# Last pair's edge columns copied on chip; edge products and folds laid between the halves of the convolutions

## The chip, the cores and the metric

The kernel runs on one core of one Trainium2 chip. The time is device microseconds (us) of one execution, the median of several. TensorE (PE in the profile) multiplies, VectorE (DVE), ScalarE (ACT) and GpSimd (POOL) do the work around it, SyncE (SP) issues transfers. Each engine takes its own instructions in the order in which they are written, and engines meet at semaphores.

## What is computed

Two levels are applied to `x`, 32 samples of 64 channels and 1024 columns. Each level is a style-modulated stack of four one-dimensional convolutions (same, upsample with blur, same, blur with downsample), then a feed-forward part whose result is added to `x`. Cut to what matters:

```python
def cond(x, style, weights, biases, mod_w, mod_b):   # one level's convs
    for i, typ in enumerate(('same', 'upsample', 'same', 'downsample')):
        x = _layer(x, style, weights[i], biases[i], mod_w[i], mod_b[i], typ)
    return x
...
x = x + L0_ffn(L0_cond(x, cond_512, ...), A, B, Wr)        # top-16 of 64 adapters of rank 16
x = x + L1_ffn(L1_cond(x, cond_512, ...), qweight, scales, zeros, bias)  # int4 weights, y = s*(q.x) - z*sum(x) + bias
```

The second level's input is the first level's output, sample by sample.

## The kernel before

**Work and tiles.** Two samples make a pair, 16 pairs a level, numbered 0 to 15 in level 0 and 16 to 31 in level 1. A pair's `x` is 128 rows (two samples of 64 channels) by 1024 columns, with even and odd columns apart, so that a convolution of one sample is a product over 128 rows (64 channels, even and odd) and 512 columns. Every float32 operand is split into a rounded part (`hi`) and a remainder (`lo`), and a product is three matmuls (hi-hi, hi-lo, lo-hi).

**Steps of a pair `c`**, by the functions of the code. `a` is the half, that is the sample, 0 or 1.
- `split`: ACT writes `x_hi`, DVE writes `x_lo` of both samples from `x_in`.
- `layer1(c, a)`: the first conv, 6 matmuls of 512 columns into `conv_ps[a]`; then ACT scales in place and writes `h_hi`, then DVE writes `h_lo` (`dve_layer1`, two instructions).
- `fold3(c)` (6 matmuls of 384) and `fold2(c)` (15 of 256): these combine the pair's remaining three convs into one set of weights. `fold_start` is the ACT and DVE work ahead of `fold3` (`v_hi`, `v_lo`). After `fold3` come `r_hi`, `r_lo`, after `fold2` come `e_hi`, `e_lo` (three ACT and three DVE instructions).
- `cond(c, a)`: the folded convs, 12 matmuls of 512 columns; ACT then writes `cond` with `act_cond`.
- `turn`, then `adapter_out` (level 0) or `quant` (level 1): 8 transposes, and the feed-forward products, 24 matmuls of 512 for each half in level 0, 16 for each in level 1. `rowsum` follows `quant`; then DVE adds bias and zero terms in `dve_second_residual`.

**Edges.** Folded convs are wrong in the first and last column. These are computed apart, for all 32 samples at once, from `x_edge`, the few outer columns of each sample: `edge_vector` steps 0 to 4 on DVE alternate with `edge_tensor` layers 0 to 3 on PE (6, 12, 6 and 18 small matmuls). Layer `k` on PE needs step `k` on DVE, which needs layer `k-1` on PE. `act_ends` copies the result into `cond`.

**Order at the change of level.** Level 1 runs three pairs ahead (`AHEAD = 3`), so pairs 16, 17, 18 and 19 go through their convs before pair 16's `quant`. Loops run over pairs 1 to 13 of level 0 and, three at a time, over pairs 17 to 28 of level 1. Between the loops everything is written out by hand. There the level-1 edge chain runs too, and level 1's weights (`quant`) are unpacked from nibbles by eight DVE and eight ACT instructions. Level 1's edge chain needs `x_edge` of all samples, so the last pair's level-0 result too: DVE writes it to `res` (`dve_first_residual`), POOL stores it to `x_scratch` in HBM (`x_after_first` in the trace), and SP loads the outer columns back with four transfers (`edge_loads`).

```python
def edge_loads(sp, s, samples):
    ...
    sp.dma_start(s.x_edge[0:C, 0, samples, 0:4], src[:, :, 0, 0:4]).then_inc(S.edges_loaded, 16)
```

The functions that the change touches follow, as they stand in the kernel before.

Of the kernel before, what the change touches and what calls it, by code (L numbers as in the profile page):

```python
# [18 lines left out]
B, C, D = 32, 64, 1024  # L19
STYLE = 128  # L20
P = 128
NPAIR = B // 2
H = D // 2
# [11 lines left out]
AHEAD = 3  # L35
# [4 lines left out]
def program(nc, t):  # L40
    with ExitStack() as outer:
        def sem(name):
            return outer.enter_context(nc.semaphore(name))
# [30 lines left out]
        S = Buffers()  # L74
        S.link = sem("link")
        S.edges_clear = sem("edges_clear")
        S.edges_loaded = sem("edges_loaded")
        S.ident_ready = sem("ident_ready")
# [190 lines left out]
        EDGES_LOADED = (16, 16 + 2 * 4 * 16)  # L269
# [189 lines left out]
        def edge_vector(v, L, s, step):  # L459
# [12 lines left out]
            if step == 0:  # L472
                V.memset(s.edge[1][hi_half, 0, 0, :], 0.0)
                V.memset(s.edge[1][lo_half, 1, 2, :], 0.0)
                v.wait_ge(S.edges_loaded, EDGES_LOADED[L])
                for side in range(2):
# [506 lines left out]
        def _(sp):  # L983
# [42 lines left out]
            edge_loads(sp, set1, slice(B - 2, B))  # L1026
# [12 lines left out]
        def _(pool):  # L1039
# [42 lines left out]
            pool.wait_ge(S.x1_stored, 16 * NPAIR)  # L1082

# [34 lines left out]
        def _(pe):  # L1118
# [74 lines left out]
            c = NPAIR + 2  # L1193
            pe.wait_ge(S.x1_ready, 2 * NPAIR + 1)
            edge_tensor(pe, 1, set1, 0)
            pe_fold2(pe, c, slot(c))
            pe_layer1(pe, c, 0, slot(c))
            pe_layer1(pe, c, 1, slot(c))
# [16 lines left out]
            for a in range(2):  # L1215
                pe_cond(pe, c, a, slot(c))
# [38 lines left out]
        def _(act):  # L1255
# [113 lines left out]
            act.wait_ge(S.x1_ready, 2 * NPAIR + 1)  # L1369
            act_nibbles(act, 6, KT)  # L1370
            for a in range(2):
                act_cond(act, c, a, slot(c))
            c = NPAIR + 2
            act_fold2(act, c, slot(c))
            for a in range(2):
                act_layer1(act, c, a, slot(c))
            act_fold_start(act, c + 1, slot(c + 1))
            split(c + 1, slot(c + 1))
            for a in range(2):
                act_cond(act, c, a, slot(c))  # L1380
            c = NPAIR + AHEAD
            act_layer1(act, c, 0, slot(c))
            act_fold3(act, c, slot(c))
            act_layer1(act, c, 1, slot(c))
            act.wait_ge(S.edges_done, 2)
            for f in range(NPAIR, NPAIR + AHEAD):
                for a in range(2):
                    act_ends(act, f, a, slot(f))
                if f == NPAIR:
                    act_turn(act, f, slot(f))  # L1390

            def second_step(i, bufs, opening=False, last=False):
                c = i + AHEAD
                if not opening:
                    act_fold_start(act, c, bufs)
                    act_turn(act, i, bufs)
                    act_layer1(act, c, 0, bufs)
                    act_fold3(act, c, bufs)
                    act_layer1(act, c, 1, bufs)
# [7 lines left out]
            second_step(FIRST, slot(FIRST), True)  # L1407
# [11 lines left out]
        def _(v):  # L1419
# [103 lines left out]
            dve_nibbles(v, 4, 6)  # L1523
            dve_first_residual(v, f, buf0)
            dve_nibbles(v, 6, KT)
            for a in range(2):
                dve_layer1(v, c, a, slot(c))
            c = NPAIR + 2
            dve_fold3(v, c, slot(c))
            raw_lo(v, 1, set1, "w2")  # L1530
            edge_vector(v, 1, set1, 0)
            split(c, slot(c))
            dve_fold2(v, c, slot(c))
            edge_vector(v, 1, set1, 1)
            for a in range(2):
                dve_layer1(v, c, a, slot(c))
            dve_fold_start(v, c + 1, slot(c + 1))
            edge_vector(v, 1, set1, 2)
            c = NPAIR + AHEAD
            split(c, slot(c))  # L1540
            edge_vector(v, 1, set1, 3)
            dve_layer1(v, c, 0, slot(c))
            dve_fold3(v, c, slot(c))
# [4 lines left out]
            def second_step(i, bufs, opening=False, last=False):  # L1548

                c = i + AHEAD  # L1550
                if not opening:
                    dve_fold_start(v, c, bufs)
                dve_turn(v, i, bufs)
                if not opening:
                    dve_layer1(v, c, 0, bufs)
                    dve_fold3(v, c, bufs)
                    dve_layer1(v, c, 1, bufs)
                    dve_reduce(v, i, bufs)
                dve_fold2(v, c, bufs)
                if opening:  # L1560
                    dve_reduce(v, i, bufs)
# [5 lines left out]
            second_step(FIRST, slot(FIRST), True)  # L1567
# [84 lines left out]
```

## Time and profile before

| | |
|---|---|
| median of 3 runs | 959.23 us (958.87 to 959.99) |
| profiled execution | 959.75 us, span 957.6 us |
| PE busy | 924.9 us, 97% of the span |
| DVE, ACT, POOL busy | 525.0, 410.6, 109.6 us |
| mean granted TensorE clock | 0.986 of full speed |

The profiled execution's time is its span and 2.15 us around it. It lies 0.5 us above the median of the runs. In the trace a row starts with its start time and its duration in us. A matmul's duration is modelled and overlaps the next one, so matmuls are best counted from start to start. Square brackets hold the engine's idle time before the row and what ended it.

### The profile page before, as it was taken

How to read it: one execution, taken by the hardware profiler on the slowest of the kernel's cores; microseconds unless marked ns; L12 is line 12 of the kernel's file. 1: busy time of each engine (PE TensorE's matmuls, PEld its weight loads, DVE VectorE, ACT ScalarE, POOL GpSimd, SP SyncE). 2: the span in 40 equal slices, each digit the busy share in tenths (PEclk: the TensorE clock that was granted, in tenths of full speed). 3: DMA queues.
4: the chain of work that ended last, by engine and by line, in shares of the span. 5: the costliest groups of instructions: out<-in, count | busy, mean ns of one | idle time of the engine just before them, and what ended most of it. 6: DMA issues, size and time to landing. Idle time of an engine off the chain costs nothing.

```text
span 957.6 us, 14271 instructions
## 1 busy us (share of the span) xinstructions
PE 924.9 (97%) x4828; PEld 812.9 (85%) x4828; DVE 525.0 (55%) x1085; ACT 410.6 (43%) x764; POOL 109.6 (11%) x140
## 2 busy tenths in 40 slices
PE   4899999999999999999999999989999999999998
PEld 4688998998998998898898898967888888888876
DVE  7795443443443343343344365567667667676666
ACT  2684234234234234234234235376454565545630
POOL 7100000000000000000000020310211121111211
PEclk8699999999999999999999999999999999999999
DMA  8701111011012011011011011342212222122111
GB/s 282 259 1 44 36 52 60 22 49 65 19 47 65 21 45 66 22 44 66 22 44 66 22 56 67 45 160 56 67 66 78 95 85 72 66 72 93 64 55 66
DMA packets 33432, 64.24 MB, mean 67 GB/s; under 512 B 12288, under 2 KB 13952, under 8 KB 33408
## 3 DMA queue, kind: packets, MB, share of 16 engines
q1 hardware_dynamic: 24336, 30.90, 10.7%
q0 software_dynamic: 9072, 33.03, 9.2%
q8 instruction: 13, 0.21, 0.1%
q14 instruction: 11, 0.09, 0.0%
HBM read 47.14 MB, written 16.78 MB: 67 GB/s over the span
## 4 chain that ended last, share of the span: by engine, by line
PE 91%; DVE 5%; ACT 2%; issue 1%; DMA 0%; SPq 0%; ACTq 0%; DVEq 0%
PE conv_ps L175 9%; PE conv_ps L177 9%; PE conv_ps L176 9%; PE prod_ps L852 6%; PE prod_ps L853 6%; PE fold_ps L613 6%; PE prod_ps L769 6%; PE prod_ps L770 6%; PE prod_ps L771 6%; PE prod_ps L751 5%; PE prod_ps L753 5%; PE prod_ps L752 5%; PE fold_ps L578 3%; PE turn_ps L724 3%; PE turn_ps L753 2%; PE turn_ps L751 2%
## 5 line engine op out<-in xcount | busy, mean ns | idle before, releaser
L161 DVE TENSOR_TENSOR h_lo<-conv_ps,h_hi 64x512 fp32r<-64x512 f32 x128 | 88.2, 689 | 47.4 <-ACT h_hi L677 46.4
L175 PE MATMUL conv_ps<-h_hi,e_hi 128*128 128x512 f32 x256 | 105.3, 411 | 3.6 <-issue 2.4
L852 PE MATMUL prod_ps<-quant,xt_hi 128*128 128x512 f32 x256 | 101.4, 396 | 2.2 <-DVE xt_lo L161 2.2
L176 PE MATMUL conv_ps<-h_lo,e_hi 128*128 128x512 f32 x256 | 102.7, 401 | 0.0
L177 PE MATMUL conv_ps<-h_hi,e_lo 128*128 128x512 f32 x256 | 102.6, 401 | 0.0
L853 PE MATMUL prod_ps<-quant,xt_lo 128*128 128x512 f32 x256 | 100.7, 393 | 0.0
L697 ACT ACTIVATE cond<-conv_ps,bias,demod_tab 128x510 f32<-128x510 f32 x64 | 49.9, 779 | 116.5 <-PE conv_ps L177 111.4
L769 PE MATMUL prod_ps<-b_hi,xt 128*128 128x512 f32 x256 | 99.8, 390 | 0.0
L770 PE MATMUL prod_ps<-b_lo,xt 128*128 128x512 f32 x256 | 99.6, 389 | 0.0
L771 PE MATMUL prod_ps<-b_hi,xt 128*128 128x512 f32 x256 | 99.6, 389 | 0.0
L751 PE MATMUL prod_ps<-a_hi,xt 128*128 128x384 f32 x256 | 87.0, 340 | 0.6 <-DVE a_lo L161 0.6
L753 PE MATMUL prod_ps<-a_hi,xt 128*128 128x384 f32 x256 | 86.5, 338 | 0.0
L752 PE MATMUL prod_ps<-a_lo,xt 128*128 128x384 f32 x256 | 86.5, 338 | 0.0
L829 DVE SCALAR_TENSOR_TENSOR res<-prod_ps,norm,res 128x512 f32<-128x512 f32 x32 | 23.9, 750 | 100.1 <-PE prod_ps L771 100.1
L730 ACT ACTIVATE xt<-turn_ps 128x512 fp32r<-128x512 f32 x32 | 17.4, 594 | 143.2 <-PE turn_ps L724 143.2
L781 ACT ACTIVATE xt<-turn_ps 128x512 fp32r<-128x512 f32 x32 | 17.4, 596 | 139.8 <-PE turn_ps L760 139.8
L161 DVE TENSOR_TENSOR xt<-turn_ps,xt 128x512 fp32r<-128x512 f32 x64 | 41.2, 686 | 65.7 <-ACT xt L781 48.9
L657 DVE SCALAR_TENSOR_TENSOR x_lo<-x_in,style_tab,x_hi 128x513 fp32r<-128x513 f32 x64 | 45.9, 759 | 54.2 <-ACT x_hi L648 54.0
L1062 POOL DMA_DIRECT2D x_after_first<-res x15 | 8.1, 542 | 480.2 <-DVE res L829 480.2
L175 PEld LDWEIGHTS conv_ps<-h_hi,e_hi 128*128 128x128 f32 x256 | 49.2, 192 | 13.7 <-issue 4.0
L177 PEld LDWEIGHTS conv_ps<-h_hi,e_lo 128*128 128x128 f32 x256 | 49.2, 192 | 11.6
L852 PEld LDWEIGHTS prod_ps<-quant,xt_hi 128*128 128x128 f32 x256 | 48.2, 188 | 12.3 <-DVE xt_lo L161 2.3
(238 smaller groups left out, 2105.6 us busy)
## 6 DMA issues: line engine op xcount, KB each, us to landing
x_in<-in_x SPq DMA_DIRECT2D x64, 128.0 KB, 2.7
res<-in_x POOLq DMA_DIRECT2D x16, 512.0 KB, 3.5
x_after_first<-res POOLq DMA_DIRECT2D x16, 512.0 KB, 2.9
x_in<-x_after_first SPq DMA_DIRECT2D x64, 128.0 KB, 2.7
res<-x_after_first POOLq DMA_DIRECT2D x16, 512.0 KB, 3.5
out_x<-res POOLq DMA_DIRECT2D x15, 512.0 KB, 3.0
a_raw<-in_adapter_in SPq DMA_DIRECT2D x8, 544.0 KB, 9.0
b_raw<-in_adapter_out SPq DMA_DIRECT2D x8, 512.0 KB, 6.5
```

The lines of the kernel that those rows point to most:

```text
L161: return nc.vector.tensor_tensor(out, whole, hi.bitcast(F32), ALU.subtract)
L175: nc.tensor.matmul(out, hi(w), moving_hi(i), start=(i == 0), stop=False)
L176: nc.tensor.matmul(out, hi(w), moving_lo(i), start=False, stop=False)
L177: last = nc.tensor.matmul(out, lo(w), moving_hi(i), start=False, stop=(i == n - 1))
L751: nc.tensor.matmul(out, bufs.xt_hi[:, k, :], bufs.a_hi[:, k, cols], start=(k == 0), stop=False)
L752: nc.tensor.matmul(out, bufs.xt_hi[:, k, :], bufs.a_lo[:, k, cols], start=False, stop=False)
L753: last = nc.tensor.matmul(out, bufs.xt_lo[:, k, :], bufs.a_hi[:, k, cols], start=False, stop=(k == KT - 1))
L769: nc.tensor.matmul(prod_ps[n][:, :], bufs.xt_hi[:, k, :], bufs.b_hi[:, k, cols], start=(k == 0), stop=False)
L770: nc.tensor.matmul(prod_ps[n][:, :], bufs.xt_hi[:, k, :], bufs.b_lo[:, k, cols], start=False, stop=False)
L771: last = nc.tensor.matmul(prod_ps[n][:, :], bufs.xt_lo[:, k, :], bufs.b_hi[:, k, cols], start=False, stop=(k == KT - 1))
L852: nc.tensor.matmul(prod_ps[n][:, :], bufs.xt_hi[:, k, :], bufs.quant[:, k, cols], start=(k == 0), stop=False)
L853: last = nc.tensor.matmul(prod_ps[n][:, :], bufs.xt_lo[:, k, :], bufs.quant[:, k, cols], start=False, stop=(k == KT - 1))
```

## The change

Three things change, all at the change of level.
1. The last pair's outer columns (samples 30 and 31) are no longer loaded from HBM by SP. DVE copies them with eight small instructions from `res`, the new function `edge_copies`; the four transfers go.
2. PE's written-out order changes: edge products and folds stand between the halves of `layer1` and `cond` where they stood ahead of or behind both halves, `layer1(17, 0)` moves ahead of the second half of `adapter_out`, and `cond(19, 0)` and `cond(19, 1)` move from behind pair 16's `rowsum` to ahead of its `quant`. ACT and DVE follow in their own order.
3. `second_step(16)`, which had a form of its own (`opening`), is written out on ACT and DVE.

```diff
-        EDGES_LOADED = (16, 16 + 2 * 4 * 16)
+        EDGES_LOADED = (16, 16 + 4 * 16)
+
+        def edge_copies(v, s, bufs):
+
+            v.wait_ge(S.x1_ready, 2 * NPAIR + 1)
+            v.wait_ge(S.edges_clear, 1)
+            for two in range(2):
+                n = B - 2 + two
+                rows = bufs.res[two * C:(two + 1) * C, :].rearrange("c (f j) -> c f j", f=2)
+                nc.vector.tensor_copy(s.x_edge[0:C, 0, n, 0:4], rows[:, 0, 0:4])
+                nc.vector.tensor_copy(s.x_edge[C:P, 0, n, 1:4], rows[:, 1, 0:3])
+                nc.vector.tensor_copy(s.x_edge[0:C, 1, n, 0:3], rows[:, 0, H - 3:H])
+                last = nc.vector.tensor_copy(s.x_edge[C:P, 1, n, 0:4], rows[:, 1, H - 4:H])
+            last.then_inc(S.edges_copied, 1)
...
             sp.wait_ge(S.x1_stored, 16 * NPAIR)
-            edge_loads(sp, set1, slice(B - 2, B))
+            sp.wait_ge(S.edges_copied, 1)
...
             pe_fold2(pe, c + 1, slot(c + 1))
+            pe_layer1(pe, c + 1, 0, slot(c + 1))
             pe_adapter_out(pe, f, buf0, 1)
 
             c = NPAIR + 1
-            for a in range(2):
-                pe_layer1(pe, c, a, slot(c))
+            pe_layer1(pe, c, 1, slot(c))
             pe_fold3(pe, c + 1, slot(c + 1))
-            for a in range(2):
-                pe_cond(pe, c, a, slot(c))
-            c = NPAIR + 2
+            pe_cond(pe, c, 0, slot(c))
             pe.wait_ge(S.x1_ready, 2 * NPAIR + 1)
             edge_tensor(pe, 1, set1, 0)
+            pe_cond(pe, c, 1, slot(c))
+            c = NPAIR + 2
             pe_fold2(pe, c, slot(c))
             pe_layer1(pe, c, 0, slot(c))
+            edge_tensor(pe, 1, set1, 1)
             pe_layer1(pe, c, 1, slot(c))
-            edge_tensor(pe, 1, set1, 1)
-            pe_cond(pe, c, 0, slot(c))
-            pe_cond(pe, c, 1, slot(c))
+            pe_fold3(pe, c + 1, slot(c + 1))
+            for a in range(2):
+                pe_cond(pe, c, a, slot(c))
+            i, c = NPAIR, NPAIR + AHEAD
+            pe_fold2(pe, c, slot(c))
+            pe_layer1(pe, c, 0, slot(c))
             edge_tensor(pe, 1, set1, 2)
-
-            i, c = NPAIR, NPAIR + AHEAD
-            pe_layer1(pe, c, 0, slot(c))
-            pe_fold3(pe, c, slot(c))
             pe_layer1(pe, c, 1, slot(c))
             edge_tensor(pe, 1, set1, 3)
+            pe_cond(pe, c, 0, slot(c))
             pe_turn(pe, i, slot(i), True)
-            pe_fold2(pe, c, slot(c))
+            pe_cond(pe, c, 1, slot(c))
             pe.wait_ge(S.quant_ready, KT)
             for n in range(2):
                 pe_quant(pe, i, n, slot(i))
             pe_rowsum(pe, i, slot(i), turn_ps[0])
-            for a in range(2):
-                pe_cond(pe, c, a, slot(c))
...
@@ vector engine, pairs 17 to 19 @@
-            dve_nibbles(v, 4, 6)
+            dve_nibbles(v, 4, 5)
+            dve_layer1(v, c, 0, slot(c))
+            dve_nibbles(v, 5, 6)
             dve_first_residual(v, f, buf0)
+            edge_copies(v, set1, buf0)
+            dve_layer1(v, c, 1, slot(c))
+            edge_vector(v, 1, set1, 0)
             dve_nibbles(v, 6, KT)
...
@@ scalar engine, pair 17 @@
+            act_layer1(act, c, 0, slot(c))
             act_nibbles(act, 4, 6)
-            for a in range(2):
-                act_layer1(act, c, a, slot(c))
+            act_layer1(act, c, 1, slot(c))
```

**PE at the first edge product.** `prod_ps0<-L1_side...` are the products of `edge_tensor` layer 0, `conv_ps...<-h...` those of `cond(17, .)`. Before:

```order
L175 MATMUL conv_ps1<-h_hi1,e_hi 128x512
L176 MATMUL conv_ps1<-h_lo1,e_hi 128x512
L177 MATMUL conv_ps1<-h_hi1,e_lo 128x512
L175 MATMUL prod_ps0<-L1_side_hi0,w1_hi 128x192 [waits lo_w1,edge_ready,x1_ready]
L176 MATMUL prod_ps0<-L1_side_lo0,w1_hi 128x192
L177 MATMUL prod_ps0<-L1_side_hi0,w1_lo 128x192
L175 MATMUL prod_ps0<-L1_side_hi0,w1_hi 128x192
L176 MATMUL prod_ps0<-L1_side_lo0,w1_hi 128x192
L177 MATMUL prod_ps0<-L1_side_hi0,w1_lo 128x192
L613 MATMUL fold_ps1<-r_hi,fold2_hi 128x256 [waits fold2_ready,fold2_hi,fold3_ready]
L613 MATMUL fold_ps1<-r_lo,fold2_hi 128x256
```

and now:

```order
L177 MATMUL conv_ps0<-h_lo0,e_hi 128x512
L178 MATMUL conv_ps0<-h_hi0,e_lo 128x512
L176 MATMUL prod_ps0<-L1_side_hi0,w1_hi 128x192 [waits lo_w1,edge_ready,x1_ready]
L177 MATMUL prod_ps0<-L1_side_lo0,w1_hi 128x192
L178 MATMUL prod_ps0<-L1_side_hi0,w1_lo 128x192
L176 MATMUL prod_ps0<-L1_side_hi0,w1_hi 128x192
L177 MATMUL prod_ps0<-L1_side_lo0,w1_hi 128x192
L178 MATMUL prod_ps0<-L1_side_hi0,w1_lo 128x192
L176 MATMUL conv_ps1<-h_hi1,e_hi 128x512 [waits layer1_ready]
L177 MATMUL conv_ps1<-h_lo1,e_hi 128x512
```

The edge product stood behind the second half of `cond(17, .)` and stands between the halves now, where half 1 is queued behind it.

**DVE from the last pair's residual to the first edge step.** `res0` is level 0's result, `nibble` a step of the weight unpacking, `h_lo` the remainder of `layer1(17, .)`. Before:

```order
L829 SCALAR_TENSOR_TENSOR res0<-prod_ps0,norm,res0 128x512 [waits out_done,res_loaded]
L829 SCALAR_TENSOR_TENSOR res0<-prod_ps1,norm,res0 128x512 [waits out_done]
L964 TENSOR_SCALAR nibble0<-packed 128x1024 [waits quant_ready]
L964 TENSOR_SCALAR nibble1<-packed 128x1024 [waits quant_ready]
L161 TENSOR_TENSOR h_lo0<-conv_ps0,h_hi0 64x512 [waits layer1_hi]
L161 TENSOR_TENSOR h_lo0<-conv_ps0,h_hi0 64x512
L161 TENSOR_TENSOR h_lo1<-conv_ps1,h_hi1 64x512 [waits layer1_hi]
L161 TENSOR_TENSOR h_lo1<-conv_ps1,h_hi1 64x512
L597 SCALAR_TENSOR_TENSOR r_lo<-fold_ps0,scale2,r_hi 128x4x64 [waits fold3_hi]
L597 SCALAR_TENSOR_TENSOR r_lo<-fold_ps0,scale2,r_hi 128x4x64
L312 SCALAR_TENSOR_TENSOR L1_w2_lo<-L1_w2_raw,L1_w2_hi 128x256 [waits hi_w2]
L473 MEMSET L1_side1 64x32
```

and now:

```order
L980 TENSOR_SCALAR nibble1<-packed 128x1024 [waits quant_ready]
L845 SCALAR_TENSOR_TENSOR res0<-prod_ps0,norm,res0 128x512 [waits out_done,res_loaded]
L845 SCALAR_TENSOR_TENSOR res0<-prod_ps1,norm,res0 128x512 [waits out_done]
L279 COPY L1_x_edge<-res0 64x4 [waits edges_clear,x1_ready]
L280 COPY L1_x_edge<-res0 64x3
L281 COPY L1_x_edge<-res0 64x3
L282 COPY L1_x_edge<-res0 64x4
L279 COPY L1_x_edge<-res0 64x4
L280 COPY L1_x_edge<-res0 64x3
L281 COPY L1_x_edge<-res0 64x3
L282 COPY L1_x_edge<-res0 64x4
L162 TENSOR_TENSOR h_lo1<-conv_ps1,h_hi1 64x512 [waits layer1_hi]
```

Eight copies follow the residual, and `h_lo1` and the first edge step (which comes next) stand ahead of the last two nibbles.

**PE from pair 16's `rowsum` on.** `turn_ps0<-sums1` is the `rowsum`, `conv_ps0<-x_hi0` is `layer1(20, 0)`, the loop's first product. Before:

```order
L838 MATMUL turn_ps0<-sums1,spread 128x1 [waits sums_reduced]
L838 MATMUL turn_ps0<-sums1,spread 128x1
L175 MATMUL conv_ps0<-h_hi0,e_hi 128x512 [waits layer1_ready,fold2_ready,fold2_hi]
L176 MATMUL conv_ps0<-h_lo0,e_hi 128x512
L177 MATMUL conv_ps0<-h_hi0,e_lo 128x512
L175 MATMUL conv_ps0<-h_hi0,e_hi 128x512
L176 MATMUL conv_ps0<-h_lo0,e_hi 128x512
```

and now:

```order
L854 MATMUL turn_ps0<-sums1,spread 128x1 [waits sums_reduced]
L854 MATMUL turn_ps0<-sums1,spread 128x1
L1248 UNCONDITIONAL_BRANCH
L1248 ISA
L681 REGISTER_ALU [waits xin_split]
L176 MATMUL conv_ps0<-x_hi0,w1_hi 128x512 [waits cond_out]
L177 MATMUL conv_ps0<-x_lo0,w1_hi 128x512
```

The 24 matmuls of `cond(19, .)` between `rowsum` and the loop are gone from here; they stand ahead of `quant` now. DVE's work behind `rowsum` is the same five instructions, and behind them, in the loop, comes `v_lo` of pair 20 as before.

## Rows read from the trace of the kernel before

**Rows 1.** The page: busy time, share of the span, instructions of each engine.

```profile
PE 924.9 (97%) x4828; PEld 812.9 (85%) x4828; DVE 525.0 (55%) x1085; ACT 410.6 (43%) x764; POOL 109.6 (11%) x140
```

**Rows 2.** Stretches (us): busy and count of each engine, granted clock, DMA.

```profile
640.00:660.00 20.00, 15.08 (x75) 12.21 (x74) 13.41 (x39) 10.22 (x17) 0.00 (x0) 0.91 0.44 145
...
700.00:720.00 20.00, 20.00 (x102) 17.01 (x101) 13.70 (x23) 11.11 (x21) 3.54 (x3) 1.00 0.23 79
```

**Rows 3.** PE in order of time at its four idle stretches: start, us, engine, line.

```profile
636.05 0.47 PE L175 MATMUL conv_ps<-h_hi,e_hi 128*128 128x512 f32 x1 [1.20 <-DVE h_lo L161]
...
641.27 0.39 PE L176 MATMUL conv_ps<-h_lo,e_hi 128*128 128x512 f32 x1
641.50 0.39 PE L177 MATMUL conv_ps<-h_hi,e_lo 128*128 128x512 f32 x1
645.27 0.33 PE L175 MATMUL prod_ps<-L_side_hi,w_hi 128*128 128x192 f32 x1 [3.37 <-issue]
...
652.24 0.33 PE L175 MATMUL prod_ps<-L_side_hi,L_turn_hi 128*128 128x128 f32 x1 [1.54 <-DVE L_side_lo L161]
...
653.64 0.61 PE L175 MATMUL conv_ps<-h_hi,e_hi 128*128 128x512 f32 x1
...
668.32 1.23 PE L724 MATMUL turn_ps<-ident,cond 128*128 128x128 f32 x8 [0.84 <-ACT cond L703]
...
678.72 0.50 PE L838 MATMUL turn_ps<-sums,spread 128*128 128x1 f32 x4
```

**Rows 4.** The chain that ended last, around the loop's start: start, us, what.

```profile
686.31 0.95 PE turn_ps L724 x8
...
688.67 1.05 PE fold_ps L578 x6
```

**Rows 5.** DVE in order of time: start, us, engine, line, what.

```profile
627.52 0.69 DVE L161 TENSOR_TENSOR e_lo<-fold_ps,e_hi 128x512 fp32r<-128x512 f32 x1 [1.75 <-ACT e_hi L625]
...
628.69 0.35 DVE L638 CAST e_lo<-e_lo 64x384 fp32r<-64x384 f32 x1
629.13 0.76 DVE L564 SCALAR_TENSOR_TENSOR v_lo<-down_T,scale,v_hi 128x192 fp32r<-128x192 f32 x2
...
634.51 1.40 DVE L161 TENSOR_TENSOR h_lo<-conv_ps,h_hi 64x512 fp32r<-64x512 f32 x2 [0.89 <-ACT h_hi L677]
...
643.71 0.67 DVE L477 TENSOR_TENSOR L_side<-L_x_edge,style_tab 128x128 f32<-128x128 f32 x2 [4.28 <-DMA L_x_edge<-x_after_first]
...
644.74 0.43 DVE L161 TENSOR_TENSOR L_side_lo<-L_side,L_side_hi 128x256 fp32r<-128x256 f32 x1
...
661.71 0.36 DVE L512 TENSOR_TENSOR L_side_scaled<-prod_ps,scale 128x192 f32<-128x192 f32 x1 [1.02 <-PE prod_ps L177]
...
662.78 0.36 DVE L161 TENSOR_TENSOR L_side_lo<-L_side,L_side_hi 128x192 fp32r<-128x192 f32 x1
...
679.25 0.16 DVE L858 TENSOR_SCALAR neg_sum<-turn_ps 128x1 f32<-128x1 f32 x1 [3.10 <-PE turn_ps L838]
...
682.16 1.23 DVE L876 TENSOR_TENSOR res<-res,scaled 128x1024 f32<-128x1024 f32 x1
```

**Rows 6.** ACT in order of time: start, us, engine, line, what.

```profile
626.85 0.58 ACT L625 ACTIVATE e_hi<-fold_ps 128x512 fp32r<-128x512 f32 x1
...
628.64 0.80 ACT L559 ACTIVATE v_hi<-down_T,scale 128x192 fp32r<-128x192 f32 x2
...
632.49 0.75 ACT L674 ACTIVATE conv_ps<-conv_ps,bias,scale 128x512 f32<-128x512 f32 x1
```

**Rows 7.** DVE's smallest forms: shapes, count, busy us, mean ns.

```profile
L797 DVE COPY scores<-prod_ps 128x64 f32<-128x64 f32 x16 | 3.6, 225 | 0.5
...
L799 DVE TENSOR_SCALAR neg_max<-top 128x1 f32<-128x1 f32 x16 | 2.5, 154 | 1.7
...
L709 DVE MEMSET h_hi<- 64x1 f32 x2 | 0.1, 59 | 0.1
```

More of the change, by code:

```diff
@@ L77, in program @@
         S.edges_loaded = sem("edges_loaded")
+        S.edges_copied = sem("edges_copied")
         S.ident_ready = sem("ident_ready")
@@ L475, in edge_vector @@
                 v.wait_ge(S.edges_loaded, EDGES_LOADED[L])
+                if L:
+                    v.wait_ge(S.edges_copied, 1)
                 for side in range(2):
@@ L1082, in _ @@
             pool.wait_ge(S.x1_stored, 16 * NPAIR)
+            pool.wait_ge(S.edges_copied, 1)
             def load_residual(f, slot):
@@ L1381, in _ @@
             c = NPAIR + AHEAD
+            act_fold2(act, c, slot(c))
             act_layer1(act, c, 0, slot(c))
-            act_fold3(act, c, slot(c))
             act_layer1(act, c, 1, slot(c))
@@ L1388, in _, with second_step @@
                     act_ends(act, f, a, slot(f))
-                if f == NPAIR:
-                    act_turn(act, f, slot(f))
-            def second_step(i, bufs, opening=False, last=False):
-                c = i + AHEAD
[L1394 to L1399, printed above, removed]
+            act_turn(act, NPAIR, slot(NPAIR))
+            act.wait_ge(S.sums_reduced, 1)
+            for a in range(2):
+                act_cond(act, c, a, slot(c))
+                act_ends(act, c, a, slot(c))
+            split(c + 1, slot(c + 1))
+            def second_step(i, bufs, last=False):
+                c = i + AHEAD
+                act_fold_start(act, c, bufs)
+                act_turn(act, i, bufs)
+                act_layer1(act, c, 0, bufs)
+                act_fold3(act, c, bufs)
+                act_layer1(act, c, 1, bufs)
                 act_fold2(act, c, bufs)
@@ L1522, in _ @@
             dve_fold_start(v, c + 1, slot(c + 1))
-            dve_nibbles(v, 4, 6)
+            dve_nibbles(v, 4, 5)
+            dve_layer1(v, c, 0, slot(c))
+            dve_nibbles(v, 5, 6)
             dve_first_residual(v, f, buf0)
+            edge_copies(v, set1, buf0)
+            dve_layer1(v, c, 1, slot(c))
+            edge_vector(v, 1, set1, 0)
             dve_nibbles(v, 6, KT)
+            c = NPAIR + 2
+            dve_fold3(v, c, slot(c))
+            split(c, slot(c))
+            edge_vector(v, 1, set1, 1)
+            raw_lo(v, 1, set1, "w2")
+            dve_fold2(v, c, slot(c))
+            dve_fold_start(v, c + 1, slot(c + 1))
             for a in range(2):
                 dve_layer1(v, c, a, slot(c))
-            c = NPAIR + 2
+            c = NPAIR + AHEAD
             dve_fold3(v, c, slot(c))
-            raw_lo(v, 1, set1, "w2")
-            edge_vector(v, 1, set1, 0)
             split(c, slot(c))
+            edge_vector(v, 1, set1, 2)
             dve_fold2(v, c, slot(c))
[L1534 to L1540, printed above, removed]
             edge_vector(v, 1, set1, 3)
             dve_layer1(v, c, 0, slot(c))
-            dve_fold3(v, c, slot(c))
             edge_vector(v, 1, set1, 4)
@@ L1546, in _, with second_step @@
             v.wait_ge(S.consts_loaded, 16 * 3)
-            def second_step(i, bufs, opening=False, last=False):
+            f = FIRST
+            dve_reduce(v, f, slot(f))
+            dve_turn(v, f, slot(f))
+            split(c + 1, slot(c + 1))
+            dve_rowsum(v, f, slot(f), turn_ps[0])
+            dve_second_residual(v, f, slot(f))
+            def second_step(i, bufs, last=False):
                 c = i + AHEAD
-                if not opening:
-                    dve_fold_start(v, c, bufs)
+                dve_fold_start(v, c, bufs)
                 dve_turn(v, i, bufs)
[L1554 to L1558, printed above, removed]
+                dve_layer1(v, c, 0, bufs)
+                dve_fold3(v, c, bufs)
+                dve_layer1(v, c, 1, bufs)
+                dve_reduce(v, i, bufs)
                 dve_fold2(v, c, bufs)
-                if opening:
-                    dve_reduce(v, i, bufs)
                 if not last:
```

18 lines of the change are left out of this document (9 added, 9 removed).

## The prediction

> **What bounds the kernel now.** I read the page first: PE is busy 97% of the span, DVE 55% [rows 1]. So only two things can pay: PE's own idle time, or PE work at a lower clock. The table of stretches then shows where they are. Both loops run without a gap, as in 700 to 720 us, with PE busy 20.00 of 20.00 and clock 1.00; at the change of level, in 640 to 660 us, PE is busy 15.08 and the granted clock is 0.91 [rows 2]. The change touches no loop body. PE's rows in order of time give the four idle stretches there: 1.20, 3.37, 1.54 and 0.84 us, 6.95 together [rows 3]. The reader is to see what each waits for. The first waits for the remainder `h_lo` of `layer1(17, 0)`. The second is the edge product of layer 0; it waits for DVE's first edge step, and that one sat idle 4.28 us until `x_edge` had come back from HBM [rows 5]. The third is edge product 1, which waits for DVE's step 1. The fourth, the transposes, waits for the end of the edge chain.
>
> A stall costs more than its bracket, since the bracket starts at a modelled end. The last matmul before the second began at 641.50, its neighbour at 641.27, and the next at 645.27 [rows 3]: 3.77 us from start to start, less one pace of 0.23, is 3.54 against 3.37. With 0.17 more each, the four cost 7.6 us. Then the clock: a mean of 0.91 over 20 us [rows 2] is 1.8 us lost. The matmul at 653.64 lasts 0.61 us where its like took 0.39 [rows 3]. By the rows this is TensorE at its lower level of 1.2 GHz, after two stalls and an edge product of 12 small matmuls. **The old change of level therefore wastes 9.4 us.** PE's work is the same in both versions, so the new time is the old one less 9.4 plus the new stalls.
>
> **What PE has to do between waits.** Paces from start to start: 0.233 a matmul of 512 columns (641.27 to 641.50), so 1.40 for a half of `layer1` (6) and 2.80 for a half of `cond` (12); edge product 1, 12 small ones, 1.40 with its restart (652.24 to 653.64), about 0.11 each, so 0.65 for one of six [rows 3]. `fold3` is 1.06 and a pair's transposes 1.0 [rows 4].
>
> **The new stalls, one by one.** Hand-overs: DVE ends at 645.17 and PE starts at 645.27, 0.1 us; from a product's last start-to-start end to ACT or DVE I take 0.25 (rowsum 678.72, DVE 679.25, less 0.34 for two tiny products) [rows 3, 5].
>
> *First edge product.* It no longer hangs on HBM. It hangs on DVE's queue, in which `h_lo1` of pair 17 stands ahead of it. From the end of `layer1(17, 1)` on PE: hand-over 0.3, ACT's layer-1 work 2.0 (632.49 to the DVE row 634.51) [rows 6, 5], `h_lo` 1.40, two memsets 0.2, edge step 0 1.46 (643.71 to 645.17) [rows 5], 0.1: 5.5 us. PE fills it with `fold3(18)` and `cond(17, 0)`, 3.86. **Stall 1.65.** Old stalls one and two together were 4.9.
>
> *The copies.* Eight new DVE instructions of 64 rows by 3 or 4 words. The trace before has none like them. From below stands a memset of 64x1 at 59 ns, from above a copy of 128x64 from PSUM at 225 ns, between them a 128x1 operation at 154 [rows 7]. I take 0.1 each, 0.8 together. They start when the residual is written, about 1.5 us after `adapter_out` ends, since one nibble and two residual instructions come first; `h_lo1` can start 3.7 us after the same moment (1.40 of `layer1`, 0.3, 2.0). The gap before it is some 2.2 us, so up to 0.27 us a copy costs nothing. Above that every 0.1 costs 0.8. If that cover were gone they would cost 0.5 to 1.8 us. The waits that they add hold up only the constants' load on SP and the residual loads on POOL, and both engines waited there for the store's landing already. Four SP transfers go, and nothing but this DVE wait hung on them.
>
> The Trainium skill, VectorE: DVE Perf Modes, section on the TRN2 errata, speaks against such copies: an instruction that reads SBUF pays a fixed cost, measured there as about 150 cycles of 0.96 GHz, however small it is. As an estimate by that page eight would take 1.3 us instead of 0.8, which the same 2.2 us would still cover; the sum would stay as it is.
>
> *Second half of pair 18.* `cond(18, 0)` needs `h_lo0` of pair 18, and ACT is busy with `fold2(18)` before it: from the end of `fold2(18)` on PE 0.3, then `e_hi` 1.79 (626.85 to 628.64), `v_hi` 0.80, layer 1 2.0 [rows 6], `h_lo` 1.40, 0.1: 6.35. PE has `layer1(18, 0)`, edge product 1, `layer1(18, 1)`, `fold3(19)`: 1.40, 1.35, 1.40, 1.06, together 5.2. **Stall 1.15.** Edge product 1 itself is ready: its DVE step, 2.05 long, starts behind `split(18)` while PE still runs `cond(17, 1)` and `fold2(18)`.
>
> *Edge product 3.* DVE does `e_lo` of pair 19 first (627.52 to 629.04, 1.52) [rows 5]. From the end of `fold2(19)`: 0.3, `e_hi`'s first instruction 0.6 [rows 6], 1.52, edge step 3 1.43 (661.71 to 663.14) [rows 5], 0.1: 3.95. PE has 1.40, 0.65, 1.40. **Stall 0.5.** The old wait of the transposes is gone, because `cond(19, 0)` stands in between.
>
> *A new place: the loop's start.* Behind `rowsum` DVE has five instructions, from 679.25 to 683.39, and then `v_lo`, 0.74, both instructions [rows 5]. `fold3(20)` needs `v_lo`. Before, PE had 24 matmuls of `cond(19, .)` and more to run in that time; now `rowsum` is followed by `layer1(20, 0)`, transposes, `layer1(20, 1)`: 0.34, 1.40, 1.0, 1.40, together 4.15. From `rowsum`'s start to `v_lo`'s end it is 4.67 and 0.74, with 0.1 5.5. **Stall 1.4**, and 0.1 more at `quant`, whose `xt_lo` comes behind `v_lo`. So a part of the gain is given back here. DVE then catches up, being busy 13.70 of 20 us in a step of the loop [rows 2].
>
> **The sum.** New stalls 1.65, 1.15, 0.5, 1.4 and 0.1: 4.8 us. 9.4 less 4.8 is 4.6. I take off 0.3, as the new order breaks PE's stream at three more places (small products between halves) and each restart costs about 0.1. That is 4.3 us: 959.75 of the profiled execution becomes 955.45. The median of the runs lies 0.5 below that execution, so 954.9, and I say **955.0 us**.
>
> **Rivals.** A difference of 0.2%, 1.9 us, is about what this measurement tells from none.
>
> *The clock falls again.* The new stalls are shorter and further apart (about 637, 650, 662 and 683 us) than the 3.37 and 1.54 that came within 10 us of each other before the fall at 653.64. Against this stands the stretch around edge product 3: the stall of 0.5 us and 18 tiny matmuls, 2.5 us with hardly any columns. The old order had the same tiny ones followed by a stall of 0.84 and kept its clock. One such fall costs 1.8 us again [rows 2]: 956.8. Chance 0.16. The Trainium skill, TensorE: Matmul & The Clock Gate, Part 1, has this rule: the array runs at half clock unless it has been busy, and idle stretches bring it back there. By that page stalls of this kind are what costs clock, and in the old trace it agrees, with 0.61 us at 653.64.
>
> *A larger gain.* DVE and ACT run earlier than I count, say because nibble 5 doesn't hold ACT, and the stalls shrink to about 3.3 us. Then 6 us are gained: 953.3. Chance 0.10.
>
> *The change does little.* The first edge product's stall stays at its old size because the DVE chain to it is longer than I count: the copies, with waits between them, take more than the 0.27 us each that is covered. At 0.4 that adds 1.1 us, at 0.7, which is the size that brings the gain near nothing, 3.4: 958.4. For it speaks only that no row shows such a copy. Chance 0.08.
>
> *Slower.* The debt at the loop's start isn't paid back: DVE enters the loop 1.5 us late, and every one of the 12 steps pays it again, up to 18 us. It would take DVE and its waits to fill the whole step, while the step shows 6.3 us free on DVE [rows 2]. It decides once the DVE lag costs over 0.5 us in each step: 961 and more. Chance 0.03.
>
> *My forecast*, 954.0 to 956.2 as its own range, has 0.63.
>
> **How the numbers follow.** The range runs from 953.2 (larger gain) to 957.4 (clock falls, with 0.6 for the copies). What lies outside is the rest of the little-gain case, the slower case, and tails of the two others, near 0.2. Faster by over 1.9 us: 0.63, 0.10, 0.13 of the clock case and 0.02 of little gain, 0.88. Slower 0.03. The same 0.09.
>
> **What the new profile would show.** Right: no `x_edge` transfer of samples 30 and 31, eight DVE copies near 634 us of 0.06 to 0.2 us each with idle DVE time behind them, PE stalls of about 1.6 us at the first edge product, 1.1 ahead of `cond(18, 0)`, 0.5 at edge product 3 and 1.4 ahead of `fold3(20)`, and a clock of 1.00 throughout 640 to 700 us. The prediction is wrong if a matmul of 512 columns lasts 0.6 us there, if the first edge product waits over 2.5 us, or if the second step of the loop still has a gap.

## The result, and the profile after

The changed kernel takes **954.65 us** (median of 8 runs, 953.55 to 957.68), the kernel before 959.93 (8 runs beside it, 958.4 to 962.41). The ratio is 0.9946, with a 95% interval of 0.9932 to 0.996: 5.3 us less, against a forecast of 955.0 in a range of 953.2 to 957.4. The profiled execution took 954.41 us with a span of 952.2, so its outside part is as large as before (2.2 against 2.15).

The table of stretches shows where the time came from (columns as in [rows 2]):

```profile
620.00:640.00 20.00, 17.86 (x91) 14.97 (x90) 16.26 (x35) 16.14 (x24) 4.67 (x6) 1.00 0.24 80
640.00:660.00 20.00, 19.09 (x108) 16.46 (x107) 16.05 (x44) 14.08 (x24) 0.00 (x0) 1.00 0.53 184
660.00:680.00 20.00, 19.78 (x103) 16.44 (x103) 10.18 (x19) 8.58 (x23) 4.76 (x2) 1.00 0.09 27
680.00:700.00 20.00, 19.00 (x95) 15.64 (x95) 15.51 (x25) 9.94 (x18) 4.09 (x4) 1.00 0.23 86
```

PE is busy 19.09 us from 640 to 660 where it was 15.08, and the granted clock is 1.00 in all four rows where it was 0.91 in one [rows 2]. PE's idle time is now in four other places. PE in order of time at each of them (first matmul behind the wait):

```profile
638.50 0.33 PE L176 MATMUL prod_ps<-L_side_hi,w_hi 128*128 128x192 f32 x1 [2.14 <-issue]
...
650.07 0.47 PE L176 MATMUL conv_ps<-h_hi,e_hi 128*128 128x512 f32 x1 [0.91 <-DVE h_lo L162]
...
661.37 0.28 PE L176 MATMUL prod_ps<-L_side_hi,L_down_hi 128*128 128x32 f32 x1 [0.22 <-DVE L_side_lo L162]
...
682.85 0.44 PE L594 MATMUL fold_ps<-v_hi,fold_hi 128*128 128x384 f32 x1 [1.00 <-DVE v_lo L580]
```

These are, in order, edge product 0, `cond(18, 0)`, edge product 3 and `fold3(20)`: the four places the prediction named. Their brackets sum to 4.27 us, against 6.95 in [rows 3]. DVE in order of time around the copies:

```profile
630.11 1.39 DVE L162 TENSOR_TENSOR h_lo<-conv_ps,h_hi 64x512 fp32r<-64x512 f32 x2 [0.84 <-ACT h_hi L693]
631.53 0.69 DVE L980 TENSOR_SCALAR nibble<-packed 128x1024 int32<-128x1024 int32 x1
632.26 1.41 DVE L845 SCALAR_TENSOR_TENSOR res<-prod_ps,norm,res 128x512 f32<-128x512 f32 x2
633.70 0.16 DVE L279 COPY L_x_edge<-res 64x4 f32<-64x4 f32 x1
633.88 0.16 DVE L280 COPY L_x_edge<-res 64x3 f32<-64x3 f32 x1
...
634.23 0.32 DVE L282 COPY L_x_edge<-res 64x4 f32<-64x4 f32 x1
...
635.10 0.17 DVE L282 COPY L_x_edge<-res 64x4 f32<-64x4 f32 x1
635.36 1.39 DVE L162 TENSOR_TENSOR h_lo<-conv_ps,h_hi 64x512 fp32r<-64x512 f32 x2
```

And ACT in order of time, in the same stretch:

```profile
632.26 1.06 ACT L985 ACTIVATE quant<-nibble 128x1024 fp32r<-128x1024 int32 x1 [1.10 <-DVE nibble L980]
633.35 0.75 ACT L690 ACTIVATE conv_ps<-conv_ps,bias,scale 128x512 f32<-128x512 f32 x1
634.13 0.59 ACT L692 ACTIVATE h_hi<-conv_ps 64x512 fp32r<-64x512 f32 x1
634.74 0.59 ACT L693 ACTIVATE h_hi<-conv_ps 64x512 fp32r<-64x512 f32 x1
```

The last copy ends at 635.27, ACT's `h_hi` at 635.33, and the waiting `h_lo` starts at 635.36. So the copies are hidden here, but with only 0.06 us left. Seven of them last 0.16 or 0.17 us and one 0.32. The reader is also to see what holds ACT: nibble 5 stands ahead of its layer-1 work, waits 1.10 us for DVE, and takes 1.06.

**The ruler for the experiments.** The span also holds differences from before the changed stretch: pair 15's transposes start at 613.43 before and at 612.17 after. So kernels are compared between two marks: the start of pair 15's transposes, and the start of pair 17's row sums in the second step of the loop, where no old or new order leaves a debt. PE's rows of before and then of after:

```profile
613.43 1.04 PE L760 MATMUL turn_ps<-ident,cond 128*128 128x128 f32 x8
...
698.60 0.50 PE L838 MATMUL turn_ps<-sums,spread 128*128 128x1 f32 x4
```

```profile
612.17 1.04 PE L776 MATMUL turn_ps<-ident,cond 128*128 128x128 f32 x8
...
693.22 0.51 PE L854 MATMUL turn_ps<-sums,spread 128*128 128x1 f32 x4
```

That is 85.17 us before and **81.05** after. The change between the marks is thus worth 4.12 us, against 4.3 in the prediction's sum. The other 1.26 of the 5.4 us by which the spans differ lies ahead of the first mark, and 1.22 of it within the first 51 us, where both kernels do the same: behind an early stall of PE 12 matmuls of 512 columns run at the lower clock in the profile of before (36.73 to 41.56 us) and 9 in this one (36.37 to 39.92). That part is not the change's. From the second mark on the two are alike: 238.20 and 238.21 us to the last row sums but one.

### The profile page after: what moved, and what is told of

It is laid out like the page before. It is cut to its first block, busy times and chain, and to the rows that moved or that the text cites. A ratio compares the mean times of both kernels' runs of the same rounds, so it can differ in the third digit from the quotient of the medians.

```text
span 952.2 us, 14279 instructions
## 1 busy us (share of the span) xinstructions
PE 922.9 (97%) x4828; PEld 810.6 (85%) x4828; DVE 526.0 (55%) x1093; ACT 410.6 (43%) x764; POOL 109.3 (11%) x140
## 4 chain that ended last, share of the span: by engine, by line
PE 90%; DVE 4%; ACT 2%; POOL 1%; issue 1%; SPq 0%; DMA 0%; DVEq 0%; ACTq 0%; POOLq 0%
PE conv_ps L176 9%; PE conv_ps L178 9%; PE conv_ps L177 9%; PE prod_ps L868 6%; PE prod_ps L869 6%; PE prod_ps L785 6%; PE prod_ps L786 6%; PE prod_ps L787 6%; PE fold_ps L629 5%; PE prod_ps L767 4%; PE prod_ps L769 4%; PE prod_ps L768 4%; PE fold_ps L594 3%; PE turn_ps L740 3%; PE turn_ps L767 2%; PE turn_ps L768 2%
```

## The experiments

Eleven runs follow, of eight new kernels and once more of the changed one. In the texts on record theory A is the reading in terms of PE's stalls, as above; what the others claim stands in each. "Between the marks" is the ruler above. Where there is one run, the marks decide and not the time. The kernels before, run beside each group, had medians of 960.94, 959.74 and 959.24 us.

**1. The copies alone**, in the old order: `edge_copies`, its semaphore and its waits from the diff above, put behind the first residual; nothing else moves.

```
-            edge_loads(sp, set1, slice(B - 2, B))
+            sp.wait_ge(S.edges_copied, 1)
...
             dve_first_residual(v, f, buf0)
+            edge_copies(v, set1, buf0)
             dve_nibbles(v, 6, KT)
```

> The kernel before, with only the eight DVE copies in place of the four transfers of samples 30 and 31; the copies stand right behind the last pair's residual, and PE's order is the old one. I measure the stretch M from the start of pair 15's transposed gates (8 transposes) to the start of pair 17's rowsum: 85.17 us before, 81.05 after. Theory A, waits counted one by one: the 1.20 us idle ahead of the conv of pair 17 grows by about 0.8 (the copies, 0.17 each in the trace after, stand ahead of h_lo), the 3.37 us idle at edge product 0 goes, since DVE's first edge step starts at about 639.6 instead of 643.7, the waits at edge product 1 (1.5) and at the transposes (0.8) stay. If the clock then stays at 1.00, M is 80.6; if it falls as before, 82.4. So the copies alone bring at least 2.7 us, and perhaps all of the 4.1. Rival B, the new order brings most of it: another wait takes the place of the one for HBM at edge product 0, M is 84 or more.

Measured: 955.1 us (6 runs, 953.35 to 957.98), ratio 0.9944, interval 0.9926 to 0.9963. Between the marks 80.99, against 81.05 with the whole change, inside the 80.6 to 82.4 of theory A and far from the 84 of rival B. PE's idle places, in order of time:

```profile
635.95 0.47 PE L176 MATMUL conv_ps<-h_hi,e_hi 128*128 128x512 f32 x1 [1.95 <-DVE h_lo L162]
...
648.53 0.33 PE L176 MATMUL prod_ps<-L_side_hi,L_turn_hi 128*128 128x128 f32 x1 [1.55 <-DVE L_side_lo L162]
...
663.27 1.23 PE L740 MATMUL turn_ps<-ident,cond 128*128 128x128 f32 x8 [0.84 <-ACT cond L719]
```

Three of the four old stalls are still there (one grown from 1.20 to 1.95). The fourth, 3.37 us at edge product 0, is gone without any reordering: that product starts at 641.64, right behind the convs. What follows: **the copies alone bring the whole gain.** The new order exchanges three stalls of 4.34 us together for four of 4.27, which is no difference.

**2. The order alone**, with the four loads from HBM kept and no copies:

```
-            sp.wait_ge(S.edges_copied, 1)
+            edge_loads(sp, set1, slice(B - 2, B))
...
-            edge_copies(v, set1, buf0)
```

> The changed kernel with the four transfers of samples 30 and 31 kept and no copies: only the new order on PE, ACT and DVE. Theory A, the order needs the copies: from the residual's end to the arrival of the edge columns it was 11.3 us before (632.4 to 643.7), and the first edge product now stands right behind the first half of pair 17's conv, with the second half queued behind it. PE then waits there some 10 us instead of 2.1: M is 88 to 91, slower than before by 3 to 6 us, and the clock may fall below 1.00 behind it. Rival B, the two parts add up independently: M is about 83, between before and after.

Measured: 965.03 us (964.37 to 965.64), ratio 1.0041, interval 1.0027 to 1.0054, so slower than before. Between the marks 91.05, 10 more than with the copies. DVE, then PE, in order of time:

```profile
644.23 0.66 DVE L491 TENSOR_TENSOR L_side<-L_x_edge,style_tab 128x128 f32<-128x128 f32 x2 [7.71 <-DMA L_x_edge<-x_after_first]
```

```profile
645.78 0.50 PE L176 MATMUL prod_ps<-L_side_hi,w_hi 128*128 128x192 f32 x1 [9.81 <-issue]
...
647.15 0.68 PE L176 MATMUL conv_ps<-h_hi,e_hi 128*128 128x512 f32 x1
...
650.19 0.63 PE L177 MATMUL conv_ps<-h_lo,e_hi 128*128 128x512 f32 x1
```

The columns come at the same moment as before (644.23 against the 643.71 of [rows 5]), but the new order asks for them earlier, so PE's wait grows from 3.37 to 9.81 us, and 8 matmuls at the lower clock follow (0.74 in 640 to 660). The two parts of the change are not additive: without the copies the order costs 5.9 us between the marks (4.1 in the medians), with them nothing.

**3. The copies twice**: the same eight again into columns that nothing reads.

```
                 rows = bufs.res[...]
+                spare = s.scaled[:, two, :, :].rearrange("p j b -> p (j b)")
+                nc.vector.tensor_copy(spare[0:C, 0:4], rows[:, 0, 0:4])
...
```

> The changed kernel with eight more copies of the same rows and sizes, written to spare columns that nothing reads, ahead of each sample's four. They cost 0.175 us each, 1.4 us together. Theory A, in the trace after DVE is busy without a gap from 630.1 to 638.4 us and the first copies already fill their cover: the idle time of PE at edge product 0 grows from 2.1 by the full 1.4, M is 82.4. Theory B, as I had counted before the result, 2.2 us of cover: 16 copies are 2.8 us, so only 0.6 is seen, M is 81.6.

Measured: 957.29 us; between the marks 83.93. DVE before and behind the sixteen copies, in order of time:

```profile
632.80 0.16 DVE L280 COPY L_side_scaled<-res 64x4 f32<-64x4 f32 x1
...
635.62 0.17 DVE L287 COPY L_x_edge<-res 64x4 f32<-64x4 f32 x1
635.81 1.39 DVE L162 TENSOR_TENSOR h_lo<-conv_ps,h_hi 64x512 fp32r<-64x512 f32 x2
```

Of the fifteen steps from 632.80 to 635.62 fourteen are 0.18 us, start to start, and one is 0.33, behind a copy of 0.32. Eight more copies at 0.178 are 1.42 us. The wait at edge product 0 is 3.52 instead of 2.14: 1.38 more, so all but 0.04 of their price shows, as theory A says. The cover was used up by the first eight. Then 8 matmuls lasted 0.6 us (639.67 to 642.66), some 1.5 us on top, which neither theory had: hence 83.93 and not 82.4.

**4. The row sums between the halves of `quant`**, twice, against the stall at the loop's start:

```
-            for n in range(2):
-                pe_quant(pe, i, n, slot(i))
+            pe_quant(pe, i, 0, slot(i))
             pe_rowsum(pe, i, slot(i), turn_ps[0])
+            pe_quant(pe, i, 1, slot(i))
```

> The changed kernel with pair 16's rowsum between the two halves of quant instead of behind both. DVE's neg_sum and the two instructions on res (1.6 us) then run while PE does the second half. Theory A, the 1.0 us idle ahead of fold3 of pair 20 is the rest of DVE's queue behind rowsum: from the end of quant to v_lo it is 3.0 us instead of 5.4, less than PE's 3.8, so the idle time goes and M falls by 1.0 to 1.2, to 79.9. Rival B, something else on DVE or ACT (x_lo of pair 20, xt_hi) holds it: M stays at 81.0.

> The kernel with rowsum between the halves of quant once more, timed. In its first trace the 1.0 us idle ahead of fold3 of pair 20 was gone, but TensorE's clock fell at 664.6 us, right behind edge product 3, and cost 1.4. Theory A, the fall belongs to the stretch of 0.2 us idle and 18 tiny matmuls, which the changed kernel has in the same form, and comes in some executions of either: in this trace it may be absent, M is then 79.8, and the median over the rounds lies 0.5 to 1.2 us under the changed kernel. Rival B, the edit itself brings it in every execution: M is 81.2 again and the median is that of the changed kernel, 954.6 or more.

Measured: 955.36, and with more runs 957.15 (952.4 to 958.08), ratio 0.9961, interval 0.9945 to 0.9978. Between the marks 81.18 and 81.30, no better than 81.05. The stall at `fold3(20)` is gone in both, as expected, but in both profiles 7 matmuls behind edge product 3 lasted 0.63 us (from 664.57 and from 664.13), and again at the last quantized products (from 923.8 and 923.4). The median of the eight runs is 2.5 us above that of the changed kernel, though the intervals of the two ratios overlap (0.9945 to 0.9978 against 0.9932 to 0.996). The time follows the run's mean granted clock: 957.14 us and more in the five runs with a clock of 0.984 or less, 954.98 and less in the three above it. Experiment 8 asks whether the edit brings the falls.

**5. Nibble 5 later**: on DVE and ACT behind the first edge step instead of ahead of the layer-1 half.

```
             act_layer1(act, c, 0, slot(c))
-            act_nibbles(act, 4, 6)
+            act_nibbles(act, 4, 5)
             act_layer1(act, c, 1, slot(c))
...
-            act_nibbles(act, 6, KT)
+            act_nibbles(act, 5, KT)
```

> The changed kernel with weight nibble 5 moved on DVE from ahead of the residual to behind the first edge step, and its ACT instruction from ahead of pair 17's second layer-1 half to behind it. In the trace after, ACT waits 1.10 us for that nibble, which stands behind h_lo on DVE, and then works 1.06 us on it before the layer-1 half; both chains reach h_lo at 635.3. Theory A, nibble 5 is what made the idle time at edge product 0 2.14 us where I had 1.65: moving it frees 0.7 us on DVE and over 0.7 on ACT, and the idle time falls by 0.7, M (from pair 15's transposes to pair 17's rowsum, 81.05 in the changed kernel, 85.17 before) to 80.4, at an even clock. Rival B, the same 0.7 us comes back behind edge product 0, in r_lo and x_lo of pair 18, which PE needs after the second half of pair 17's conv: M stays at 81.0 and a wait of 0.5 us or so appears ahead of fold2 or layer 1 of pair 18.

Measured: 953.51 us; 80.35 between the marks, 0.70 less. ACT in order of time: its layer-1 work now starts when PE is done.

```profile
630.03 1.06 ACT L985 ACTIVATE quant<-nibble 128x1024 fp32r<-128x1024 int32 x1
632.51 0.75 ACT L690 ACTIVATE conv_ps<-conv_ps,bias,scale 128x512 f32<-128x512 f32 x1 [1.42 <-PE conv_ps L178]
```

The first stall is 1.42 us instead of 2.14, the others as they were. The edit takes the nibble out of both queues, so it does not say which of them counted. On DVE the copies now end at 634.32 and `h_lo` starts at 634.53, 0.21 us later, when ACT is done.

**6. `v_hi` of pair 19 earlier** on ACT, ahead of pair 17's last `cond` instead of ahead of pair 18's layer 1, where it took 0.80 us out of the chain to `cond(18, 0)`.

```
+            act_fold_start(act, c + 2, slot(c + 2))
             act_cond(act, c, 1, slot(c))
             c = NPAIR + 2
             act_fold2(act, c, slot(c))
-            act_fold_start(act, c + 1, slot(c + 1))
```

> The changed kernel with ACT's v_hi of pair 19 (0.8 us) moved from between fold2 and layer 1 of pair 18 to ahead of pair 17's last cond instruction, where ACT waits 1.19 us. Theory A, ACT's queue alone makes the 0.91 us idle ahead of pair 18's conv (fold2 1.8, v_hi 0.8, layer 1 2.0): it falls by 0.7 to 0.8, M from 81.05 to 80.3 at an even clock. Rival B, DVE's e_lo and v_lo hold h_lo instead: under 0.3 us gained.

Measured: 953.53 us; 80.30 between the marks, 0.75 less, and no wait is left at `cond(18, 0)`.

**7. All three edits together.**

> The changed kernel with all three edits, rowsum between the halves of quant, nibble 5 late, v_hi of pair 19 early. Theory A, each wait is of its own: M is 81.05 less 1.2, 0.7 and 0.8, 78.4 us at an even clock, and the time 2.7 us under the changed kernel, near 952.0. A fall of the clock like the one at 664.6 us in the run with rowsum early (7 matmuls of 0.6 us) takes 1.4 back: 953.4. Rival B, the waits are coupled through DVE, which is then nearly full from 630 to 645 us: M 79.5 or more.

Measured: 953.07 us (6 runs, 951.51 to 954.6), ratio 0.9923, interval 0.9909 to 0.9937; 79.62 between the marks, with stalls of 1.46 and 0.22 only, but also 8 slow matmuls from 662.23 on. Its ratio is the lowest of the study, 6.7 us below its kernel before, but its interval overlaps that of the changed kernel, which was measured beside other runs, so the times alone don't show that it is faster.

**8. Does the clock fall because of the moved row sums?** Three kernels on one chip: two of the edits without the row sums, all three again, and the changed kernel again.

> The changed kernel with two of the three edits: nibble 5 behind the first edge step, and v_hi of pair 19 ahead of pair 17's last cond on ACT; the row sums stay behind both halves of quant. From pair 15's transposes to pair 17's row sums the changed kernel took 81.05 us. The two edits alone took 0.70 and 0.75 off, so both theories expect 79.6 us with stalls of about 1.4, 0, 0.2 and 1.0. They differ on the clock, which in all three profiles with the row sums moved had fallen behind edge product 3 (7 or 8 matmuls of 0.6 us) and again at the last quantized products. Theory E (the moved row sums bring it): no slow matmul here, and a time of about 953.0, no more than all three edits. Theory P (when it falls is a matter of the moment, not of this edit): slow matmuls may stand here too, then 81.1 us and 1.5 more at the end.

> The same kernel as with all three edits, one more profile. Theory E (the moved row sums bring the clock's fall): slow matmuls behind edge product 3 and at the last quantized products again, 79.6 us between the two marks and some 239.7 from the row sums of pair 17 to the last but one. Theory P (the moment decides): with a chance near one half at least one of the two falls is gone, then 78.1 and 238.2.

> The changed kernel itself, one more profile. Theory E (a clock fall comes with the moved row sums only): no slow matmul at 620 to 720 us or at the last quantized products, 81.05 us between the two marks. Theory P (the moment decides): a fall is possible at either place, 1.5 us each.

Measured: two edits 954.15 us (5 runs, 952.2 to 955.23), ratio 0.9949, interval 0.9934 to 0.9963; 79.52 between the marks, no slow matmul behind edge product 3 or at the end. The 1.5 us that the marks show are not seen in the ratio, which is that of the changed kernel (0.9946): the profiled run, 952.2 us with a mean clock of 0.991, is the fastest of the five, and the other four have 0.987. All three again 952.08 and 78.08 between the marks: the fall behind edge product 3 is gone, the one at the end is there. The changed kernel again 956.06, with both falls. Its PE rows behind edge product 3, in order of time:

```profile
660.80 0.28 PE L176 MATMUL prod_ps<-L_side_hi,L_down_hi 128*128 128x32 f32 x1 [0.22 <-DVE L_side_lo L162]
...
662.83 0.48 PE L176 MATMUL conv_ps<-h_hi,e_hi 128*128 128x512 f32 x1
663.15 0.39 PE L177 MATMUL conv_ps<-h_lo,e_hi 128*128 128x512 f32 x1
...
664.14 0.63 PE L178 MATMUL conv_ps<-h_hi,e_lo 128*128 128x512 f32 x1
...
666.70 0.63 PE L178 MATMUL conv_ps<-h_hi,e_lo 128*128 128x512 f32 x1
```

Between the marks it took 694.19 − 611.66 = 82.53 us, 1.48 more than the same program in the first profile (81.05). Behind edge product 3 theory E is refuted in both directions: the fall comes without the edit (here), and stays away with it (all three again). So the edit doesn't decide it alone. Whether it makes falls more frequent is open. Behind edge product 3 they stand in 3 of 4 profiles with the row sums moved and in 1 of 5 without (those with copies and new order and no earlier fall); at the last quantized products in all 4 with them moved and in 3 of 9 without.

## Why the prediction was right, and where a term was off

**The sum held, partly by luck.** The forecast was 4.3 us of gain in this stretch, and 4.12 were measured. The four stalls came where they were said to, but their errors and those of two other terms have different signs and cancel, as the following shows. The time came out at 954.65 against 955.0, though the medians of eight runs differ by 5.3 us and not 4.3: the kernel before stands at 959.93 in these runs, 0.7 above the 959.23 from which the forecast was worked out.

**First edge product: forecast 1.65 us, came 2.14 in the bracket, 2.3 from start to start.** This is the mis-sized term, 0.65 too small. PE in order of time, from the product behind `layer1(17, 1)` to the last of `cond(17, 0)`:

```profile
632.37 0.33 PE L594 MATMUL fold_ps<-v_hi,fold_hi 128*128 128x384 f32 x1
...
635.97 0.39 PE L178 MATMUL conv_ps<-h_hi,e_lo 128*128 128x512 f32 x1
```

The step that failed is "hand-over 0.3" from PE's last matmul of `layer1(17, 1)` to ACT. PE was done at 632.37 and ACT started at 633.35, 0.98 later, since nibble 5's `quant` held ACT until 633.32. All behind it came as worked out: 2.01 us of layer 1, 1.35 to the memsets, 1.47 for edge step 0. But ACT was not alone. DVE was late by as much: its copies ended at 635.27, 0.06 before ACT was done, so a free ACT would have gained next to nothing. The prediction let the residual end 1.5 us behind `adapter_out`; it ended 2.7 behind (633.67, where the product behind `adapter_out` starts at 630.97), since `h_lo` of the first half ran until 631.50 and nibble 5 until 632.22 ahead of it. The prediction's count had no nibble 5 in ACT's sum, and named no `h_lo` of the first half in DVE's. Experiment 5 takes the nibble out of both: ACT starts 0.26 us after PE is done, near the 0.3 of the forecast, the stall is 1.42 and 0.70 us are gained.

**The copies: forecast 0.1 us each, took 0.16 to 0.17 (one 0.32), and 1.66 from the first start to the next instruction.** The conclusion "costs nothing" held, but narrowly and by luck: two errors met. The gap for them was 635.33 − 633.70 = 1.63 us, not 2.2, so the stated limit of 0.27 us a copy was 0.2, and had ACT been ready after the forecast 0.3 the gap would have been 0.95 and a part of the copies would have shown. Idle DVE time behind them, which the prediction expected to see, there was none, and experiment 3 shows that the next copy is paid in full. The estimate from the Trainium skill, VectorE: DVE Perf Modes, section on the TRN2 errata (about 150 cycles for each small instruction that reads SBUF), was the better one, and this case's rows agree with it: 0.16 us is 154 cycles of 0.96 GHz.

**`cond(18, 0)`: forecast 1.15, came 0.91 (1.07 from start to start).** Right, and for the reason given: with `v_hi` out of ACT's chain (experiment 6) the stall is gone.

**Edge product 3: forecast 0.5, came 0.22 (0.4).** **`fold3(20)`: forecast 1.4 and 0.1 more, came 1.00 (1.17) and nothing more.** Both in their place and a little smaller. Together the small errors cancel the large one: from start to start the four are 4.93 us against the forecast 4.8.

**The clock and the restarts: 1.8 and 0.3 us, both too large.** The old fall cost 8 matmuls of 0.43 us from start to start (653.64 to 657.03, 3.39 us) instead of 0.233, so 1.5 us; the 1.8 came from a mean clock of two digits. Old waste is then 7.6 and 1.5, new stalls are 4.93, and the difference of 4.2 is less than 0.1 above the 4.12 measured: that is what is left for the three more places at which PE's stream is broken, where 0.3 was taken off.

**What the sum hid.** It was made over the whole stretch, old waste less new stalls, and so it could not say which part of the change earns what. Experiments 1 and 2 do: the copies earn all of it, by the stall at edge product 0 and the fall of the clock behind it, and the order alone loses 0.4%.

**The rival "the clock falls again" was not beaten, it happens in some executions.** It named edge product 3 as the place, and there the fall stood in 4 of 9 profiles of kernels with copies and new order that had not fallen earlier, in the changed kernel itself in one of two. It costs 1.48 us there, against the 1.8 taken from [rows 2]. So the prediction's own sign of being wrong, a matmul of 512 columns of 0.6 us in this stretch, is absent from the first profile and present in the second. The first stands at 954.41 us with a mean granted clock of 0.989, the second, with two falls, at 956.06 with 0.987. Of the eight runs behind the median, six have 0.989 (953.55 to 955.34 us), and 0.985 and 0.986 go with the two slowest (956.3 and 957.68). The median thus lies among the six with the higher clock, though 0.989 doesn't exclude one fall: the profile of all three again has that clock and the fall at the end. Two profiles don't measure the chance, and 0.16 is neither confirmed nor refuted.

**The other rivals.** "A larger gain" was priced for the case that nibble 5 doesn't hold ACT, but the sum itself, with its hand-over of 0.3, had already taken ACT as free, so this rival had no gain of its own. Nibble 5 held ACT, and with it moved 0.7 us came, not 1.5. "The change does little" asked for copies of 0.4 us with waits between them; they follow each other at 0.18. For "slower" there is nothing: the second step of the loop runs without a gap.

## What to carry to other kernels

When a change both removes a late transfer and reorders the work around its wait, measure the two apart: here the removal alone was the whole gain, and the same order with the transfer kept was a loss. A new order has to be judged by its own stalls, which here summed to as much as those that it replaced. When an instruction is placed in a gap of another engine's queue, count what each queue that meets there still has ahead of the instruction that ends the gap (here one nibble, on DVE and on ACT, 0.7 us), and expect the gap to end all at once. Where a kernel stalls on PE, one profile doesn't show its clock: the same program may or may not lose 1.5 us in the same place. The mean granted clock of each run tells where a profile stands among them.

## What the runs showed of the hardware

- Small copies on VectorE within SBUF, 64 rows by 3 or 4 words, take 0.16 to 0.17 us and follow each other at some 0.18 us (one of the eight took 0.32, and one of the sixteen in experiment 3); the nearest rows ahead of the change were 0.15 for a 128x1 operation and 0.06 for a memset [rows 7].
- The clock after a given stall is not the same every time. At the last quantized products PE waits 2.18 us in all 13 profiles, behind the same transposes and row sums. In 7 of them the products behind it run at the lower level (0.63 us a matmul instead of 0.40), in 6 not. The kernel before was of the second kind. PE in order of time, first of the changed kernel's first profile, then of its second:

```profile
923.00 0.51 PE L868 MATMUL prod_ps<-quant,xt_hi 128*128 128x512 f32 x1 [2.18 <-DVE xt_lo L162]
923.34 0.40 PE L869 MATMUL prod_ps<-quant,xt_lo 128*128 128x512 f32 x1
```

```profile
923.98 0.79 PE L868 MATMUL prod_ps<-quant,xt_hi 128*128 128x512 f32 x1 [2.18 <-DVE xt_lo L162]
924.57 0.63 PE L869 MATMUL prod_ps<-quant,xt_lo 128*128 128x512 f32 x1
```

- Before the fall at 664.14 PE had waited 0.22 us, run 18 matmuls of 32 columns (2.0 us), and then full-size ones for 1.3 us at the upper level: the fall doesn't come at once. The Trainium skill, TensorE: Matmul & The Clock Gate, Part 1, speaks of idle time as what brings the lower clock; here it also came where PE had been idle for 0.22 us only, with the 18 small matmuls behind it, and stayed away behind 2.14 us. What decides between the executions stays open: no run here shows it.
